# First self attention: thresholds 2 and 3 of a quad in the odd steps, the sums of both halves behind them, both copies in the next even step

## What is computed

```python
q = (X @ W_Q + b_Q) ; k, v = ...            # q, k rotated (rope)
scores = einsum('bhtd,bhsd->bhts', q, k) * ATTNSCALE
w = softplus(scores / sqrt(key_self))       # causal: 0 for later keys
w = w * sigmoid(SCALE * w)
w = where(w < sinks, 0.0, w)                # one threshold for each head
total = sum(w, axis=-1) + sinks + 1e-6
out = einsum('bhts,bhsd->bhtd', w / total, v) + sinks / total * v_null
y = (context @ W_O + W_O_bias).mean(over the 4 branches)
```

## Time and profile before

| | us |
|---|---|
| median of 3 runs | 3142.68 |
| lowest to highest | 3139.65 to 3147.96 |
| the profiled execution | 3136.61 |
| its span | 3134.8 |
| granted TensorE clock, mean | 0.929 |

### The profile page before, as it was taken

One profiled execution on the slowest core, in us unless ns is written; L12 is line 12 of the kernel. 1 busy time (PEld: TensorE's weight loads), 2 busy tenths in 40 slices (PEclk: granted clock), 3 DMA queues, 4 the chain that ended last, 5 costly groups with the idle time before them and its releaser, 6 DMA issues. The chain is left out here.

```text
span 3134.8 us, 49356 instructions
## 1 busy us (share of the span) xinstructions
PE 2737.2 (87%) x17088; PEld 2032.4 (65%) x17088; DVE 1967.2 (63%) x4294; ACT 1714.7 (55%) x3164; POOL 705.2 (22%) x814
## 2 busy tenths in 40 slices
PE   6778888888867689999979999999978999959998
PEld 3344444544435556776758888888867877748887
DVE  4788778778865756655645665666666565555444
ACT  3887887878864444444435555555546555542221
POOL 1122212222210144444430000000004665610000
PEclk8789889988878899999989999999989999979999
DMA  3000000000001111111020000000010000020000
GB/s 102 4 4 4 0 3 3 0 3 3 1 0 52 67 46 24 24 38 32 21 61 1 1 1 1 1 1 1 1 66 8 5 8 5 1 95 7 7 3 30
DMA packets 85089, 57.70 MB, mean 18 GB/s; under 512 B 54672, under 2 KB 74512, under 8 KB 84432
## 3 DMA queue, kind: packets, MB, share of 16 engines
q1 hardware_dynamic: 84944, 55.79, 5.9%
HBM read 39.00 MB, written 8.39 MB: 15 GB/s over the span
## 5 line engine op out<-in xcount | busy, mean ns | idle before, releaser
L1912 POOL TENSOR_SCALAR x_weights<-x_weights,x_sums 128x256 f32<-128x256 f32 x256 | 231.9, 925 | 872.0 <-DVE x_sums L1971 872.0
L672 DVE SCALAR_TENSOR_TENSOR a_w<-a_w,a_sinks 128x384 f32<-128x384 f32 x512 | 332.7, 714 | 32.0 <-ACT a_w L507 32.0
L1125 POOL TENSOR_SCALAR f_weights<-f_weights,f_sums 128x256 f32<-128x256 f32 x256 | 232.1, 924 | 272.8 <-DVE f_sums L1355 272.8
L486 ACT ACTIVATE a_e<-psum 128x1024 f32<-128x1024 f32 x192 | 195.6, 1019 | 155.4 <-PE psum L345 114.6
L1557 ACT ACTIVATE a_turned_w_hi<-psum 128x512 fp32r<-128x512 f32 x256 | 139.0, 595 | 195.0 <-PE psum L1491 195.0
L1283 ACT ACTIVATE f_weights<-psum,f_negmax 128x256 f32<-128x256 f32 x256 | 118.0, 473 | 215.2 <-DVE f_negmax L1349 215.2
L687 DVE SCALAR_TENSOR_TENSOR a_w<-a_e,psum 128x512 f32<-128x512 f32 x256 | 162.8, 676 | 92.1 <-ACT a_e L488 87.3
L342 PE MATMUL psum<-a_qT,a_kT_half 32*128 32x512 f32 x512 | 164.9, 723 | 60.4 <-DVE a_w L687 49.3
L1621 DVE TENSOR_REDUCE a_negmax<-psum 128x1 f32<-128x1024 f32 x128 | 156.7, 1224 | 89.8 <-PE psum L123 89.8
L488 ACT ACTIVATE a_e<-a_e 128x1024 f32<-128x1024 f32 x192 | 203.0, 1057 | 6.1
L1882 ACT ACTIVATE x_weights<-x_masked_s,x_negmax 128x256 f32<-128x256 f32 x256 | 127.0, 497 | 136.2 <-DVE x_negmax L1963 136.2
(11 more groups left out here) (335 smaller groups left out, 7354.6 us busy)
## 6 DMA issues: line engine op xcount, KB each, us to landing
f_xnT<-all_xnT_all SPq DMA_DIRECT2D x16, 256.0 KB, 2.3
f_pv_rows<-f_pv SPq DMA_DIRECT2D x8, 512.0 KB, 3.1
f_pv_groups<-f_pv_rows SPq DMA_DIRECT2D x8, 512.0 KB
f_w<-in_f_w SPq DMA_DIRECT2D x2, 2048.0 KB, 9.7
all_x_all<-in_x SPq DMA_DIRECT2D x1, 2048.0 KB, 8.3
a_wq<-in_a_wq SPq DMA_DIRECT2D x2, 1024.0 KB, 10.4
a_wo<-in_a_wo SPq DMA_DIRECT2D x2, 1024.0 KB, 12.3
a_xnT<-all_xnT_all SPq DMA_DIRECT2D x8, 256.0 KB, 2.3
```

The lines of the kernel that those rows point to most:

```text
L486: act.activation(e[:, x, :], psS[x], ACT.Exp).then_inc(exp_done, 1)
L672: ins = dve.scalar_tensor_tensor(part, part, sinks[:, col:col + 1], part, ALU.is_ge, ALU.mult)
L1125: ins = pool.tensor_scalar(w, w, sums[:, k, h, t:t + 1], None, ALU.mult)
L1912: ins = pool.tensor_scalar(w, w, sums[:, k, h, t:t + 1], None, ALU.mult)
```

## The change

DVE does only thresholds 0 and 1 in the even step, at points 1 and 2. Thresholds 2 and 3 stand in the following odd step, behind the caps of slots 0 and 1 (points 0 and 1). PE sums both halves behind each other in the odd step, after the scores of slots 0 and 1 and what is sent there, ahead of the scores of slot 2 (which in this program are those of the next, even, step). ACT copies both halves in the next even step, behind slot 0. `SUM_BANKS` and what waits for them are turned round to fit; five takes of DVE move with their banks: regroup 2 from point (0, 0) to (7, 1) of the batch before, regroup 5 from (2, 0) to (1, 1), the key norm from (4, 0) to (3, 1), query 1 ahead from (6, 0) to (5, 1). What each instruction computes stays.

```diff
--- before.py
+++ after.py
@@ -223,16 +223,16 @@
 SENT_LATE = {0: ("regroup", 4, OLD, 6), 1: ("regroup", 5, OLD, 7), 2: ("regroup", 7, OLD, 6), 3: ("norm", 0, AHEAD, 7),
              4: ("q", 0, AHEAD, 7), 5: ("q", 1, AHEAD, 6), 6: ("q", 3, AHEAD, 7), 7: ("regroup", 2, HERE, 6)}
 
-SUM_BANKS = {1: (7, 6), 3: (7, 6), 5: (6, 7), 7: (6, 7)}
+SUM_BANKS = {1: (6, 7), 3: (6, 7), 5: (7, 6), 7: (7, 6)}
 
 EVEN_POINTS, ODD_POINTS = 6, 3
-TAKEN = {(0, 0): ("regroup", 2, OLD, 6), (0, 1): ("regroup", 3, OLD, 7), (0, 2): ("q", 0, HERE, 6), (0, 3): ("q", 1, HERE, 7),
+TAKEN = {(0, 1): ("regroup", 3, OLD, 7), (0, 2): ("q", 0, HERE, 6), (0, 3): ("q", 1, HERE, 7),
          (0, 4): ("q", 2, HERE, 6), (0, 5): ("q", 3, HERE, 7), (1, 0): ("regroup", 4, OLD, 6),
-         (2, 0): ("regroup", 5, OLD, 7), (2, 1): ("k", 0, AHEAD, 6), (2, 2): ("k", 1, AHEAD, 7), (2, 3): ("v", 0, HERE, 6),
+         (1, 1): ("regroup", 5, OLD, 7), (2, 1): ("k", 0, AHEAD, 6), (2, 2): ("k", 1, AHEAD, 7), (2, 3): ("v", 0, HERE, 6),
          (2, 4): ("regroup", 6, OLD, 7), (3, 0): ("regroup", 7, OLD, 6),
-         (4, 0): ("norm", 0, AHEAD, 7), (4, 4): ("regroup", 0, HERE, 6), (5, 0): ("q", 0, AHEAD, 7),
-         (6, 0): ("q", 1, AHEAD, 6), (6, 3): ("out", 0, OLD, 6), (6, 4): ("regroup", 1, HERE, 7), (6, 5): ("q", 2, AHEAD, 6),
-         (7, 0): ("q", 3, AHEAD, 7)}
+         (3, 1): ("norm", 0, AHEAD, 7), (4, 4): ("regroup", 0, HERE, 6), (5, 0): ("q", 0, AHEAD, 7),
+         (5, 1): ("q", 1, AHEAD, 6), (6, 3): ("out", 0, OLD, 6), (6, 4): ("regroup", 1, HERE, 7), (6, 5): ("q", 2, AHEAD, 6),
+         (7, 0): ("q", 3, AHEAD, 7), (7, 1): ("regroup", 2, HERE, 6)}
 REGROUPS = 8
 ROTATED = 2 + 2 * BR
 
@@ -379,7 +379,7 @@
 
                 free.clear()
                 if old:
-                    free.update({6: (regroup_taken, (b - 1) * REGROUPS + 3), 7: (sums_taken, ((b - 1) * QUADS + 2) * 2 + 2)})
+                    free.update({bank: (sums_taken, ((b - 1) * QUADS + 2) * 2 + half + 1) for half, bank in enumerate(SUM_BANKS[7])})
                 elif new:
                     free.update({6: (rot_made, b * ROTATED + 5), 7: (rot_made, b * ROTATED + 6)})
 
@@ -438,8 +438,9 @@
                 for step in range(PAIRS_OF_HEADS):
                     quad = quad_at(b, (step - 3) // 2, new, old) if step % 2 else None
                     for x in range(SLOTS):
-                        if x < 2 and quad:
-                            sum_half(b, quad, x, SUM_BANKS[step][x])
+                        if x == 2 and quad:
+                            for half in range(2):
+                                sum_half(b, quad, half, SUM_BANKS[step][half])
                         if step < PAIRS_OF_HEADS - 1 and new:
                             score_slot(b, step + 1, x)
                         elif step == PAIRS_OF_HEADS - 1 and ahead:
@@ -487,7 +488,8 @@
                             act.wait_ge(exp_done, n + 1)
                             act.activation(e[:, x, :], e[:, x, :], ACT.Ln, bias=1.0).then_inc(ln_done, 1)
                         if step % 2 == 0 and x == 0:
-                            take_sums(quad_at(b, step // 2 - 2, new, old), 1)
+                            for half in range(2):
+                                take_sums(quad_at(b, step // 2 - 2, new, old), half)
                         if old and (step, x) == (4, 1):
                             take_turned(2)
                             take_turned(3)
@@ -510,8 +512,6 @@
                             take_turned(1)
                         if quad:
                             act.preload_act_table_set("natural_log_exp_and_others")
-                        if step % 2 and x == 2:
-                            take_sums(quad_at(b, (step - 3) // 2, new, old), 0)
 
             over_batches(act, body)
 
@@ -695,17 +695,17 @@
             def body(b, new, ahead, old):
                 exists = {HERE: new, AHEAD: ahead, OLD: old}
                 for step in range(PAIRS_OF_HEADS):
-                    silu_quad = quad_at(b, step // 2 - 1, new, old) if step % 2 == 0 else None
+                    silu_quad = quad_at(b, step // 2 - 1, new, old)
                     for point in range(ODD_POINTS if step % 2 else EVEN_POINTS):
                         x = point if step % 2 else {0: 0, 4: 1, 5: 2}.get(point)
                         if x is not None and new:
                             cap(b, step, x)
-                        if silu_quad and 1 <= point <= 3:
+                        if silu_quad and step % 2 == 0 and 1 <= point <= 2:
                             threshold(silu_quad, point - 1)
+                        if silu_quad and step % 2 and point <= 1:
+                            threshold(silu_quad, 2 + point)
                         if (step, point) in TAKEN and exists[TAKEN[step, point][2]]:
                             take_from_spare(b, *TAKEN[step, point])
-                    if silu_quad:
-                        threshold(silu_quad, 3)
 
             over_batches(dve, body)
```

## The result

The changed kernel takes 3210.6 us (median of 4 runs, 3204.1 to 3223.7) beside 3142.3 for the kernel before: a ratio of 1.022, with an interval of 1.0185 to 1.0256. The forecast was 3167, the range ended at 3207. So it is slower, as forecast, but by 68 us and not by 24, and the time lies 4 us outside the range.

The account below looks back on a forecast made before the run. No engine is full; engines wait in turn, and the chain from O decides. Rounds 0, 2, 4, 6 give +14.7, -13.6, +19.2 and +3.2, +0.8: +24.3 us on 3136.6 is 3161, plus 6 for the median: 3167, range 3132 to 3207.

Parts of the forecast that it names:

- O: End of the odd step's first slot on ACT; the change was said to affect only what follows it.
- one chain of caps, thresholds and sums: From O to the next table load nothing overlaps: 10.5 us plus a take; chance 0.62, 3167 us.
- round 4: Steps 4 and 5; late projection ahead of the sums and lost slack: tail 12.5 from 9.3, +3.2 us.
- round 2: Steps 2 and 3; cap of even slot 1 earlier, threshold 3 meets POOL: tail 13.0 from 14.7, -1.7 us.
- round 0: Steps 0 and 1; four projections delay DVE's odd cap 0 to O + 2.5: tail 13.8 from 11.7, +2.1 us.
- rival 3: PE's clock falls to half (1.2 of 2.4 GHz) before the sums in two rounds of four: +40, 3207 us; chance 0.13.
- round 6: Steps 6 and 7; late DVE and POOL's work beside the thresholds: tail 13.0 to 13.3 from 13.1, +0.1 us.
- tails: Each round's time from O to ACT's next silu table load; sum 48.8 us a batch before, forecast +3.7.
- The meeting with POOL: Round 2: threshold 3 beside POOL's four context operations, 2.89 us, was to grow by 1.4 us.
- The copies at nothing: Copies of both halves move behind even slot 0 on ACT; no cost was forecast for the move itself.
- Rival 2: Early cap wins in all rounds and no moved threshold meets POOL: -3.5 us a batch, 3116 us; chance 0.14.
- Rival 4: Nothing measurable: round 2's gain recurs in round 6, round 4 loses half: +0.4 us a batch, 3146; chance 0.11.

Follow-up runs that it names:

- the filled change: Changed kernel with repeated matmuls in PE's waits of all four rounds, and 2, 5, 5 added ones in steps 1, 3, 5: 3168.7 us, 1.009.
- the run with this round as before: Changed kernel with steps 4 and 5 (thresholds, sums, copies, take of query 1) as in the kernel before: 3186.8 us, 1.0134.
- the filled kernel before: Kernel before the change with repeated matmuls in PE's waits (query 1, regroup 6, turned contexts, projections ahead of the next scores): 3126.0 us, 0.9926.
- the run with one place filled: Changed kernel with the value projection repeated once and regroup 6 twice, in PE's two waits of round 2 alone: 3207.6 us, 1.0184.
- the fill of ten matmuls: Changed kernel with PE's waits filled in all rounds, plus 4, 10, 10 matmuls between scores 0 and 1 in steps 1, 3, 5: 3197.0 us, 1.0173.
- the best version: Kernel before with PE's waits filled (regroup 6 run 3 times, not 6) and threshold 2 behind the caps in step 2 alone: 3108.6 us, 0.989.

## Why the prediction was right or wrong

**The direction: right; the mechanism: right in part.** After O one chain of caps, thresholds and sums ends the round, and ACT waits for the sums 17.8 us a batch (forecast 12 to 20), while its wait for slots 0 and 1 fell from 13.3 to 5.1. Of the signs by round only one came: round 4 is longer, but round 2 is not shorter and round 0 is not longer.

**The step that failed is PE's clock.** The chain was priced at full clock in every round (both halves of the sums 2.95 us), and half clock was set aside as rival 3, with a chance of 0.13 and the reason "the new gaps are of 1 to 2 us", beside a gap of 0.92 us that had done nothing. In round 2 the gaps are of that size, 1.75 and 1.36 us, but there are two of them 2 us apart, and the clock fell behind them; in round 6 the gap is 2.51 us. I had looked for gaps before the sums, where I had priced them; they stand before the scores, behind a threshold and behind POOL. Rival 3 named two rounds in four and 3207 us, 4 us short of what was measured. That it comes so near is in part luck: it put 2.5 us on the sums of each such round, and they took 1.3 and 1.7 us more than 2.79; the rest is scores and the key norm at half clock, which it did not name, and losses of the order in round 4 that the kernel before, with its own half clock, had hidden. By the Trainium skill (TensorE: Matmul & The Clock Gate, "A second HAM failure mode: psum-queue depth-cycling") short idle times between groups of matmuls make the clock swing and cost throughput. These traces agree in that: rounds 2 and 6 ran at 0.77 and 0.84, and filling the idle time gave back 42 us. The kernel that the Trainium skill tells of there cycles through PSUM banks. This one waits for other engines, and here the cost is in a chain.

**What the half clock costs, in numbers.** In the repeating batch it is 116.0 - 108.6 = 7.4 us for the change, 2.8 of it in round 2 and 4.6 in round 6, and nothing in round 4, which is 29.7 us at 0.83 as at 0.94. For the kernel before it is 109.2 - 105.8 = 3.4, 1.4 in round 2 and 2.0 in round 4. Each is a lower bound, since the added matmuls cost time too and the filled kernels' rounds still hold some lower clock; their difference, 4.0, is then an estimate and no bound. By this batch the +6.8 is 2.8 of order and 4.0 of clock. By the medians order has the greater part (above). The profiled executions of the two filled kernels, 3158.6 and 3131.5 us, are 27 apart, near the forecast's 24, but that is chance: the one was the fastest of its four and the other the slowest of its six.

**The forecast, round by round.** Its tails were made with sums of 2.95 us, PE at full clock, so the filled change is the one to hold it against; but the lengths to which it added them, those of before, held a half clock of their own. Two clocks were mixed in one sum: the rounds it gives, 27.3, 30.0, 27.5 and 28.1, are 112.9 us, where the filled change takes 108.6 and the change itself 116.0.
- Round 4: +3.2 forecast, +2.9 measured; 30.0 and 29.7 us. The slack of the kernel before was lost for the reason given, and the run with this round as before gave 3.6 back in it. The size is luck in part: with both kernels filled the round loses 4.9 us, since the one before had 2.0 us of half clock in it.
- Round 2: -1.7 forecast, +0.2 measured. Without the half clock it is 26.4 us, where the forecast had 27.3. The meeting with POOL was sized too high: threshold 3 took 2.92 us beside 1.85 of POOL, 0.72 more than the 2.20 of threshold 2 without it, and not 1.4 more. POOL was slowed as well: its two multiplications, 1.85 us here, took 1.20 in round 0 without a threshold beside them. The Trainium skill (SBUF — State Buffer, "Who interferes with whom") calls the contention of the two engines an exclusive lock. By that an estimate of the growth is POOL's own 1.20 us, not its 1.85, which holds its own waiting; measured is 0.72, so the trace shows contention on both sides, but less than a full lock. The 2.89 us that the prediction compared with held such waiting too: those four operations took 3.16 us there and 1.33 + 1.20 in round 2. Windows of the changed kernel from the start to the end of either threshold (the ends of their neighbours reach in, so six and five records):

```profile
442.68:444.88 2.20, 2.20 (x6) 1.01 (x6) 2.20 (x6) 1.44 (x2) 0.00 (x0) 0.50 0.00 0
446.97:449.89 2.92, 2.78 (x7) 1.28 (x8) 2.92 (x5) 2.05 (x2) 1.85 (x2) 0.50 0.00 0
```

- In round 2 also, the key norm took 1.91 us (half clock) and the sums 4.05, not 2.95: this made up for what the forecast had put too high.
- Round 6: +0.1 forecast, +3.9 measured. The sentence that PE puts out the next batch's scores only when POOL has added the projection behind threshold 2 was right; it was given no price of its own. It is a wait of 2.51 us where it had been 1.5, and then scores at 2.08 us and sums at 4.49. Without half clock the round is 26.7 us, the forecast had 27.5.
- Round 0: +2.1 forecast, -0.2 measured. "DVE starts odd cap 0 at O + 2.5" failed: it was there at O + 0.8 (416.46, O being 401.32 + 14.3). ACT's wait, which was to stay at 2.97 us, became 1.32. The forecast's time for the fourth projection came from a round with a clock of 0.93, where two of the projections had run slowly (2.08 and 1.65 us); this one had 1.00.

**The copies at nothing**: right, 0.9996.

**Rival 2**, faster by the early cap in all rounds, fell. In round 2 it held, some 2 us while the sums stayed ahead, and 1.2 in the filled change against the filled kernel before (at clocks of 1.00 and 0.88).

**Rival 4** fell with round 6.

**Slips in the working.** The chain of round 4 adds up to O + 8.86, not 8.95. The chances by their own rule are slower 0.69 and same 0.17, not 0.72 and 0.14. Neither moves the forecast.

**Still open.** Rounds take one of a few lengths (round 4: 29.7, 31.4 or 34.4 us) and change between them from batch to batch, with the same instructions; in the run with one place filled the 34.4 have the lowest clock, 0.65, against 0.77 and 0.78. Which of the gaps decides was not taken apart further. The filled change with round 4 as before, which the table by rounds points to, was not run. Why the later stages took from 2178 to 2196 us was not tried.

## What to carry to other kernels

Where PE is one of several engines that wait for each other in turn, ask of each reordering where PE will stand idle and which matmuls follow, and price that chain at both clock levels; the idle places of the whole period count, not the one beside the edit. Before crediting or blaming an order, run both versions with PE's waits filled by repeats of matmuls that write the same numbers: that parts the order from the clock, roughly (here +2.8 and +4.0 us in the repeating batch, and more order than that by the medians), and may be a gain by itself (0.9926). Keep the fill no longer than the wait: here the fill of ten matmuls was 28 us slower than the one of five. And try a moved step at each of its places singly: threshold 2 late was a gain of some 2 us in one round and, without the fills, a loss in two others.

## What the hardware did that was not expected

- A wait of 2.51 us was followed by half clock (above), but one of 2.98 us was not, while one of 2.59 us at the same projections in the kernel before was. Round 0 of the changed kernel, timeline of PE, and then one row of the kernel before:

```profile
407.72 1.03 PE L400 MATMUL psum<-all_xnT_all,a_wqs 128*128 x4
411.73 1.13 PE L400 MATMUL psum<-all_xnT_all,a_wq 128*128 x4 [2.98 <-DVE a_rot L621]
412.69 1.03 PE L400 MATMUL psum<-all_xnT_all,a_wqs 128*128 x4
```

```profile
494.49 2.08 PE L400 MATMUL psum<-all_xnT_all,a_wq 128*128 x4 [2.59 <-DVE a_rot L621]
```

In the best version the same wait of 2.07 us, behind the same instructions, was followed by either clock. So in these traces the length of one gap does not decide, and the row with 0.92 us was a weak reason.
- More matmuls made the kernel faster: 484 more PE records in 560 us, and 21.7 us less in all.
- Repairs of one round alone (three runs) lengthened other rounds of the repeating batch by about as much as they gained, or more. The time still fell by 24 us in one of them, in the first and last batches and in later stages.
